# One maxima tile per half step on all 128 rows instead of 64

## The reference, cut to what matters

```python
qk = einsum('bhqd,bhkd->bhqk', q, k) * scale       # att1, att2: keys after the query are masked out
p = softmax(qk, axis=-1)
p = p * triu(ones)                                 # att0 only: masked after the softmax
z = einsum('bhqk,bhkd->bhqd', p, v)
```

## Time and profile before

| | us |
|---|---|
| median of 3 runs (2870.03 to 2876.72) | 2876.49 |
| profiled execution, its own time | 2868.02 |
| its span, first to last instruction | 2866.3 |
| `att0`, from its first k load to its last scores | about 73 to 857 |
| `att1` | about 956 to 1402 |
| `att2` | about 1689 to 2150 |

### The profile page before, as it was taken

The page is one execution under the profiler, slowest core; times in us unless marked ns, Lnnn a source line. Parts: engine busy times, 40 slices in busy tenths (PEclk is TensorE's granted clock), DMA queues, the critical chain, the costliest instruction groups (busy, mean ns, idle before and its releaser), DMA issues. The chain is left out here.

```text
span 2866.3 us, 40334 instructions
## 1 busy us (share of the span) xinstructions
PE 2437.6 (85%) x14416; PEld 1102.3 (38%) x14416; DVE 1971.5 (69%) x3999; ACT 1431.5 (50%) x2105; POOL 380.0 (13%) x559
## 2 busy tenths in 40 slices
PE   4799999999974699999779959999996879787997
PEld 2333333333321343333334324333332356433663
DVE  4888888888824788888445558988855645455553
ACT  1067676676761046777422214677762246422662
POOL 2000000000000200001200010001121423122330
PEclk8599999999996689999879967999986779887998
DMA  5400100000000501212100051021222433033320
GB/s 182 56 8 11 21 11 11 7 11 6 4 4 29 118 10 26 41 26 46 27 1 0 2 128 27 11 35 27 45 45 59 112 111 113 19 101 100 113 98 15
DMA packets 88118, 130.26 MB, mean 45 GB/s; under 512 B 30608, under 2 KB 52752, under 8 KB 85904
## 3 DMA queue, kind: packets, MB, share of 16 engines
q1 hardware_dynamic: 78496, 109.10, 16.1%
q10 hardware_dynamic: 9456, 18.99, 2.4%
HBM read 59.16 MB, written 13.63 MB: 25 GB/s over the span
## 5 line engine op out<-in xcount | busy, mean ns | idle before, releaser
L700 ACT ACTIVATE att_probs<-psum 128x1024 f32<-128x1024 f32 (+3 forms) x1152 | 1037.6, 951 | 614.7 <-PE psum L748 613.3
L658 DVE TENSOR_REDUCE att_part_max<-psum 128x1 f32<-128x512 f32 x1792 | 1127.4, 683 | 161.1 <-PE psum L730 157.2
L730 PE MATMUL psum<-k_rows,att_q_rows 64*128 64x512 f32 (+3 forms) x2304 | 819.0, 482 | 101.7 <-DMA att_q_rows<-q_pieces 37.7
L730 PEld LDWEIGHTS psum<-k_rows,att_q_rows 64*128 64x128 f32 x2304 | 360.3, 196 | 756.6 <-DVE att_part_max L658 534.3
L773 PE MATMUL psum<-att_probs,v_aug 128*9 128x512 f32 (+3 forms) x3712 | 443.3, 552 | 19.2 <-ACT att_z_sb L692 19.0
L748 PE MATMUL psum<-att_q_rows,k_rows 64*128 64x512 f32 (+3 forms) x2304 | 419.3, 406 | 14.5 <-ACT att_probs L700 10.2
L655 DVE CUSTOM_DVE_ANT_0 att_masked<-psum,mask_max_sb 128x384 bf16<-128x384 f32 (+3 forms) x512 | 232.8, 486 | 79.2 <-PE psum L730 74.2
L748 PEld LDWEIGHTS psum<-att_q_rows,k_rows 64*128 64x128 f32 x2304 | 238.5, 193 | 89.8 <-ACT att_probs L700 59.7
L608 POOL TENSOR_SCALAR_AFFINE_SELECT att_probs<-att_probs 128x256 f32<-128x256 f32 x256 | 102.5, 406 | 809.4 <-ACT att_probs L700 807.0
L1378 ACT ACTIVATE latt_probs<-psum,latt_bias,latt_scale 128x192 f32<-128x192 f32 x256 | 127.3, 507 | 120.2 <-DVE latt_bias L1417 120.2
L769 PE MATMUL psum<-att_probs,att_one_only 128*9 128x512 f32 (+3 forms) x1280 | 147.8, 534 | 10.1 <-ACT att_z_sb L692 10.0
(11 more groups left out here) (259 smaller groups left out, 2488.9 us busy)
## 6 DMA issues: line engine op xcount, KB each, us to landing
k_rows<-k_pieces SPq DMA_DIRECT2D x96, 256.0 KB, 8.2
latt_k<-local_k_T SPq DMA_DIRECT2D x32, 384.0 KB, 3.0
att_q_rows<-q_pieces SPq DMA_DIRECT2D x168, 64.0 KB
lproj_table<-in_tables SPq DMA_DIRECT2D x16, 512.0 KB, 4.3
lproj_swapped<-lproj_other SPq DMA_DIRECT2D x128, 64.0 KB, 2.0
lproj_swapped<-lproj_other ACTq DMA_DIRECT2D x128, 64.0 KB, 2.2
latt_q<-local_q_T SPq DMA_DIRECT2D x32, 256.0 KB, 2.4
latt_v_own<-local_v_tok SPq DMA_DIRECT2D x32, 256.0 KB, 2.3
```

The costliest lines, as they stand in the source:

```text
L658: nc.vector.tensor_reduce(column, ring[e % NRING][:, 0:w], AX.X, ALU.max).then_inc(ring_free, 1)
L700: nc.scalar.activation(probs[s % NPROBS][:, pr, :, at:BANK], st[pr][:, :, at:BANK], ACT.Exp, scale=scale).then_inc(st_free, 1)
L730: nc.tensor.matmul(ring[e % NRING][:, 0:w], q_rows[u % NQ][rows, pr, qt * P:(qt + 1) * P].bitcast(F32R), k_rows[b][rows, pr, kc * BANK:kc ...
```

## The change

A second copy of q is kept: `q_alone`, two buffers of 128 partitions by 2 (`i`) by 2 (`pr`) by 512, in which part `i` holds the q rows of half `i` and zeros on all other partitions. It is loaded per unit from unit 1 on (`load_alone`, four more DMAs of 64 KB on SyncE's queue). The last maxima tile ahead of a step's products, if it is of a unit after the first, takes its weights from there and runs on 128 rows against both halves of k; the other half's products with zero add nothing. The other maxima tiles stay on 64 rows. `zeros` becomes a part of `q_alone[0]` that stays zero.

```diff
+        q_alone = [sb(f"q_alone{b}", [P, 2, 2, BANK]) for b in range(2)]
...
-        zeros = sb("zeros", [16, P])
+        zeros = q_alone[0][64:80, 0, 0, 0:P]
...
+            def load_alone(u):
+                g, c = units[u]
+                if u == 1:
+                    sp.wait_ge(alone_clear, 4)
+                if u == 2:
+                    sp.wait_ge(spare_clear, 4)
+                for i in range(2):
+                    for a in range(2):
+                        rows = slice(64 * i + 16 * a, 64 * i + 16 * a + 16)
+                        piece = q_dram[a, c].rearrange("(g i d p) s -> g i d (p s)", g=NG, i=2, p=2)[g, i]
+                        sp.dma_start(q_alone[u % 2][rows, i, :, :].rearrange("r p s -> r (p s)"),
+                                     piece.unsqueeze(1).to_broadcast([HD, 2, 2 * BANK])).then_inc(alone_in[u % 2], 16)
...
             load_k(1)
+            load_alone(1)
             put_max(0)
             load_q(3)
             load_k(2)
-            sp.wait_ge(fill_set, 1)
+            sp.wait_ge(spare_clear, 4)
             for u, (g, c) in enumerate(units):
+                if u + 2 < NU:
+                    sp.wait_ge(ring_full, plan.done_at[u])
+                    load_alone(u + 2)
                 if u + 1 < NU:
                     put_max(u + 1)
...
             pool.wait_ge(more_clear, MORE)
+            for i in range(2):
+                for half in range(2):
+                    nc.gpsimd.memset(q_alone[1][64 * half:64 * half + 64, i, :, :], 0.0).then_inc(alone_clear, 1)
+            pool.wait_ge(alone_clear, 4)
...
-            nc.vector.memset(zeros[:, :], 0.0).then_inc(fill_set, 1)
+            for i in range(2):
+                for half in range(2):
+                    nc.vector.memset(q_alone[0][64 * half:64 * half + 64, i, :, :], 0.0).then_inc(spare_clear, 1)
...
-            def maxima(count):
+            def maxima(count, products_next=False):
...
-                        nc.tensor.matmul(ring[e % NRING][:, 0:w], q_rows[u % NQ][rows, pr, qt * P:(qt + 1) * P].bitcast(F32R),
+                        if products_next and e == count - 1 and u > 0:
+                            pe.wait_ge(alone_in[u % 2], QIN * ((u + 1) // 2))
+                            weights, rows = q_alone[u % 2][:, i, pr, qt * P:(qt + 1) * P], slice(0, P)
+                        else:
+                            weights = q_rows[u % NQ][rows, pr, qt * P:(qt + 1) * P]
+                        nc.tensor.matmul(ring[e % NRING][:, 0:w], weights.bitcast(F32R),
...
-                maxima(plan.issued_by(u, (kb + 0.5) / plan.blocks[u]))
+                maxima(plan.issued_by(u, (kb + 0.5) / plan.blocks[u]), s >= 2)
                 if s >= 2:
                     products(s - 2)
```

More of the change, by code:

```diff
@@ L501, in attention @@
         q_in = [sem(f"q_in{b}") for b in range(NQ)]
+        alone_in = [sem(f"alone_in{b}") for b in range(2)]
+        alone_clear = sem("alone_clear")
+        spare_clear = sem("spare_clear")
         m_in = [sem(f"m_in{b}") for b in range(NQ)]
         z_out = [sem(f"z_out{b}") for b in range(2)]
-        fill_set = sem("fill_set")
         rows_clear = sem("rows_clear")
```

## The result

The change makes the kernel slower: 2938.98 us, median of 4 runs (2935.14 to 2941.34), against 2876.6 for the kernel before (4 runs). The ratio is 1.0214, 95% interval 1.0184 to 1.0243, so about 62 us. The forecast was 2960, its range 2910 to 2990. The sign and the main cause came out; the forecast's sum was 90 us, and 62 were measured.

A forecast was written before the change was run, and what follows sets the result against it. A loop through both TensorE and VectorE was taken to bound the attention stages. Stands 59, drains 23, clock 7 and start 1 made 90 us more, giving 2958 or 2966.5, stated as 2960; range 2910 to 2990.

The forecast's parts named there:

- The stands: TensorE waiting for late q_alone copies, mainly at the causal stages' ends: 59 us in all, bounds 18 and 67.
- rival 1: In SyncE's queue the copy overtakes k, so stands are only 9.1 and 8.5 us: 2920 us; chance 0.18.
- unit 14: Short late unit of the third stage: its first changed tile waits 17.4 us for a copy landing behind k.
- The drain: Added before 128-row tiles after 64-row ones, where pairs could go at once: 23 us, bounds 14 and 27.
- The clock behind the stands: TensorE's clock may fall to 1.2 GHz after long waits: 7 us, bounds 0 and 15.
- The products' drain: Between last maxima tile and products: remains with a 128-row tile, tile to products staying 0.42 us, gain 0.
- rival 2: Products' weights load under the 128-row tile, giving back up to 86 us; chance 0.07 faster, 0.03 about even.
- the rows of the transpose: Trace of the 128-row transpose of the maxima: products' weights load only 0.08 us before its end, so it drains.
- The tile at half rate: The 128-row maxima tile streams at half rate, adding 106 us; not expected.
- rival 3: The 128-row tile streams at half rate: 106 us on top, 3066 us; chance 0.03.
- Copy, memsets and SyncE's queue: Extra loads and memsets at the stages' starts, mostly hidden: 1 us.
- two starting points: Profiled execution of 2868.0 us and median of 2876.5: plus 90 us they give 2958 and 2966.5, hence 2960.

The follow-up runs named there:

- e1_early: The changed kernel with each q_alone copy issued one turn earlier, ahead of that turn's zeros, q and k: 2887.28 us, ratio to before 1.0036.
- e4_wide_only: The kernel before with the same tiles on 128 rows of the one q, no copy or wait, exponential's scale 1e-6: 2879.13 us, ratio 1.0002.
- e3_unused: The changed kernel with copies and memsets made, but no tile using or awaiting them, tiles on 64 rows: 2879.89 us, ratio to before 1.0005.
- e5_scale: The kernel before with only the exponential's scale set to 1e-6: 2878.74 us, ratio to before 1.0015.
- e2_wait_64: The changed kernel with copies, memsets and waits kept, but the tile back on 64 rows of the old q: 2936.32 us, ratio to before 1.0208.
- e7_covered: e1_early with 64-row tiles again in turns 14 and 15 of the first stage and 3, 4, 5, 6, 9 of the causal ones: 2869.34 us.
- e6_between: Against e1_early, the copy issued between the turn's q and k instead of ahead of zeros, q and k: 2900.24 us, ratio to before 1.0086.

## Why the prediction was right, and where its sum was off

**The stands were the cause, as said.** Expected 59 us, measured 48.6, of which 47 in the causal stages' ends. The chain was right in each link: the tile asks while SyncE is at the zeros, the copy lands last, behind k, by 1.65 us (taken: 2), and e1_early, which takes the waits away, takes away 51 of the 62 us. The Trainium skill, DMA: Bandwidth & Descriptors, Queues, rings and completion order, says that each DMA engine consumes descriptors in the order of its ring, while completion is not first in, first out. The trace agrees as far as it goes: here the 256 KB behind the 1 MB of k landed last. So rival 1, the copy overtaking k with 2920 us and stands of 9.1, falls. The terms were too large: unit 14's 15.7 instead of 17.4, because TensorE, delayed by what comes earlier, asks 1.2 us later against SyncE's queue (4.7 us before the last k issue, not 5.9); units 13 and 11, 5.8 and about 2 instead of 6.5 and 3.5; unit 2, 0.8 and 0.9 instead of 1.5; and unit 15, which did not wait.

**The drain was the step that failed, by its size.** The price of one place was right (0.42 us taken; e4_wide_only shows 0.39 to 0.42 at the 30 places). The sum read off was 26.7 us of TensorE, and I let "nearly all" pass on, 23. By turns it is 18. The same reading, done by turns, gives some 4 us each for turn 14 of the first stage and turn 6 of each causal one, and those grew by 2.4; turn 12, some 2 us read off, grew by 1. What e4_wide_only's turn lengths show is the sum; that the missing 9 us of TensorE go where TensorE would next have waited for ScalarE is read from turn 14 of the first stage alone, where TensorE's idle time ahead of the scores fell from 3.6 us to 1.4.

**The clock behind the stands** was about the 7 us taken. Turns 9, 11 and 12 of the change, less their waits, are together 10 us longer than e1_early's over the two stages (11 if e1_early's waits of 1.0 us are taken out too), turns 14 are 3 us shorter, and turns 13 and 15 differ by 0 in one stage and 3.5 in the other: 7 to 11 us.

**What the sum had not at all** is that 128-row tiles keep the clock up before the ends. Taken over whole stages, the two kernels with such tiles and no stand (e1, e4) are 7 us longer than the three with 64-row tiles (before, e3, e5; means of the stage lengths), not 18: 11 come back, 4 of them in the falls counted above, the rest in the first and last turns, whose lengths scatter by 2 to 3 us from one execution to the next, so that this part is not shown to be the tiles' doing. The medians agree within their width: e1_early is 7.4 us over e3_unused, the change 2.7 over e2_wait_64, e4_wide_only 1.3 over before, each figure some 4 to 6 us to either side. That the 128-row tiles raise the granted clock is shown (e4_wide_only against e5_scale); how many of the 11 us that gives back is not.

**The parts taken at nothing.** The products' drain: 426 against 423 ns, so rival 2 falls and with it its 86 us; full width before 9 columns still drains, as the rows of the transpose said. The tile at half rate: 0.49 us, so rival 3 falls. Copy, memsets and SyncE's queue: 2 us at most (e3_unused).

**The sum as it stands.** By the profiles 49 for the stands, 7 to 11 for the clock behind them, some 7 for the drains less what the clock gives back, 2 for the copy: 65 to 69, for 62 measured. The medians leave less for the second: e1_early takes away the first two, 51 us with 47 of waits (9.5 us left). e7_covered takes away the third as well (nothing left). The forecast of 2960 was nearer than its sum, for it lay between two starting points; from the median of 2876.5 the sum gave 2966.5.

## What to carry to other kernels

A buffer that is loaded a turn before its unit can still be late where another engine runs two units ahead: find for each new load the earliest instruction that reads it, and what stands ahead of it in the queue, at the short units above all. A tile that takes all rows costs nothing behind a wait for a bank, and its whole length where it ends the run of two tiles side by side. And price such an edit by turns: here the delays read off instruction by instruction, 26.7 us, were an upper bound on the 18 by which the turns grew.

## What the runs showed of the hardware that was not expected

- TensorE, equally busy (18.6 of 20 us), was granted 0.91 of its clock with 64-row tiles and 1.00 with a fifth of them (506 of 2304) on 128 rows; 11 falls to 1.2 GHz in three profiles against 2 in four, and a median of 0.884 against 0.893 over 12 runs each of e5_scale and e4_wide_only. Why, no run here settles: e4_wide_only shows only that it needs neither the copy nor its loads.
- Two 64-row tiles, one on each half, and the scores behind them load within 0.11 us; with one of the two on 128 rows it is 0.86 us. The Trainium skill, TensorEngine Tiling (Array Packing), Key Properties, lets a change of tiling mode drain TensorE; here that and the lost pair are worth 0.43 us a step, 7 us a turn.
- A DMA of 64 KB behind nothing but q took some 4.2 us from its issue to the tile's start (e6_between: four issues from 1383.04 on, 0.67 us apart, so the last at about 1385.1; the tile runs at 1389.30). The last two k DMAs of 256 KB, each behind two or three of their own kind, took 7.9 and 9.3 in the change.
